# The key-bias term of each query in block B: from a TensorE row product to VectorE sums over row buffers

## The reference

```python
h = film(rmsnorm(x, norm1_w), cond, film1_w, film1_b)
Q = h @ q_w + q_b
K = h @ k_w + k_b
V = h @ v_w + v_b
scores = jnp.einsum('bnd,bmd->bnm', Q, K) * D ** (-0.5)
attn = jax.nn.softmax(scores, axis=-1)
out = jnp.einsum('bnm,bmd->bnd', attn, V)
x = x_in + (out @ proj_w + proj_b)
h = film(rmsnorm(x, norm2_w), cond, film2_w, film2_b)
h = jax.nn.gelu(h @ mlp_w1 + mlp_b1, approximate=False) @ mlp_w2 + mlp_b2
```

## Time and profile before

| | |
|---|---|
| median of 3 runs | 1538.35 us (1538.13 to 1538.81) |
| the profiled execution | 1537.32 us, its span 1535.4 us |
| TensorE busy | 1515.0 us (99%) |
| VectorE, ScalarE, GpSimd busy | 788.4, 592.9, 581.4 us |
| DMA | 117.87 MB, mean 77 GB/s |

### The profile page before, as it was taken

How to read it: one execution, slowest core, us unless ns; L and a number is a source line. 1 busy time by engine, 2 the same in 40 slices (tenths; PEclk the granted TensorE clock), 3 DMA queues, 4 the chain that set the end, 5 groups by cost and what they waited for, 6 DMA issues and landing times.

```text
span 1535.4 us, 24533 instructions
## 1 busy us (share of the span) xinstructions
PE 1515.0 (99%) x8992; PEld 1235.9 (80%) x8992; DVE 788.4 (51%) x1616; ACT 592.9 (39%) x1884; POOL 581.4 (38%) x504
## 2 busy tenths in 40 slices
PE   5999999999999999999999999999999999999999
PEld 4888888888887668888788888888888888888887
DVE  5677777777766675555546342332524233252522
ACT  4656565656554446555554221211212121121210
POOL 5656666676654545443553311021211102121100
PEclk9999999999999999999999999999999999999999
DMA  7122222222126234333343220020201002020100
GB/s 252 63 80 87 80 93 77 96 77 91 58 81 232 71 138 158 97 103 126 122 127 114 69 69 15 1 82 0 75 7 68 14 1 81 0 75 7 55 1 28
DMA packets 60237, 117.87 MB, mean 77 GB/s; under 512 B 6352, under 2 KB 10448, under 8 KB 60144
## 3 DMA queue, kind: packets, MB, share of 16 engines
q1 hardware_dynamic: 60144, 116.65, 22.4%
HBM read 91.33 MB, written 25.30 MB: 76 GB/s over the span
## 4 chain that ended last, share of the span: by engine, by line
PE 97%; POOL 1%; DVE 1%; DMA 1%; SPq 0%; issue 0%
PE bank L587 27%; PE bank L589 27%; PE bank L588 27%; PE bank L666 4%; PE bank L659 2%; PE bank L677 2%; PE bank L963 2%; PE bank L884 1%; PE bank L718 1%; PE bank L709 1%; PE bank L611 1%; PE bank L987 1%; POOL xa L1746 1%; DMA xa<-xt_in 1%; PE bank L906 1%; PE bank L966 0%
## 5 line engine op out<-in xcount | busy, mean ns | idle before, releaser
L1705 DVE CAST g_hi<-gf 128x512 fp32r<-128x512 f32 x128 | 68.7, 537 | 427.1 <-ACT gf L1271 427.1
L1271 ACT ACTIVATE gf<-bank,cols 128x512 f32<-128x512 f32 x128 | 88.3, 690 | 512.6 <-PE bank L589 512.6
L1106 ACT ACTIVATE pa<-bank,neg_max 128x128 f32<-128x128 f32 x512 | 181.7, 408 | 135.5 <-DVE neg_max L1378 135.5
L587 PE MATMUL bank<-w_hi,g_hi 128*128 128x512 f32 x512 | 200.5, 392 | 0.0
L587 PE MATMUL bank<-hb_hi,w_hi 128*128 128x512 f32 x512 | 199.4, 389 | 0.3 <-DVE vb_lo L1294 0.3
L589 PE MATMUL bank<-w_hi,g_lo 128*128 128x512 f32 x512 | 199.4, 389 | 0.0
L588 PE MATMUL bank<-w_lo,g_hi 128*128 128x512 f32 x512 | 199.2, 389 | 0.0
L589 PE MATMUL bank<-hb_hi,w_lo 128*128 128x512 f32 x512 | 199.2, 389 | 0.0
L588 PE MATMUL bank<-hb_lo,w_hi 128*128 128x512 f32 x512 | 199.2, 389 | 0.0
L1781 POOL TENSOR_TENSOR pa<-pa,rec 128x512 f32<-128x512 f32 x128 | 143.2, 1126 | 56.2 <-DVE rec L1401 56.1
L1755 POOL TENSOR_TENSOR xrc<-xrc,b 128x512 f32<-128x512 f32 x32 | 48.7, 1550 | 303.0 <-DMA xrc<-x_dram 302.9
(11 more groups left out here) (201 smaller groups left out, 3132.6 us busy)
## 6 DMA issues: line engine op xcount, KB each, us to landing
rows<-st_dram SPq DMA_DIRECT2D x32, 512.0 KB, 4.3
xb<-x_dram SPq DMA_DIRECT2D x60, 256.0 KB, 2.9
xa<-xt_in SPq DMA_DIRECT2D x32, 256.0 KB, 4.4
xra<-xt_in SPq DMA_DIRECT2D x32, 256.0 KB, 2.7
x_dram<-h SPq DMA_DIRECT2D x32, 256.0 KB, 2.0
xrb<-x_dram SPq DMA_DIRECT2D x32, 256.0 KB, 3.3
stage_w<-w_in SPq DMA_DIRECT2D x16, 512.0 KB, 3.8
x_dram<-xrb SPq DMA_DIRECT2D x32, 256.0 KB, 2.2
```

The lines of the kernel that those rows point to most:

```text
L587: nc.tensor.matmul(dst, w_hi, a_hi, start=start, stop=False)
L1106: last = nc.scalar.activation(pa[:, j, m, :], scores_bank[j][:, m * P:(m + 1) * P], ACT.Exp, bias=neg_max[:, j * C + m:j * C + m + 1], acc ...
L1271: nc.scalar.activation(gf[f % 2][:], bank[f % 2][:], ACT.Gelu, bias=cols[:, B1_COL + f:B1_COL + f + 1])\
L1705: nc.vector.tensor_copy(g_hi[:, r, :], gf[f % 2][:]).then_inc(g_hi_ready, 1)
```

## The change

From group 1 on, `h_u`, the copy to rb and the fifth score product are left out; group 0 keeps them. In their place the key-bias term is summed on VectorE: for sequence t, the row u_t = scale_t * uc (512 numbers) is written to DRAM once (`u_dram`, made in group 0 by four multiplications or sums on VectorE, `u_transpose` on TensorE and a copy on ScalarE), loaded to all partitions by SP into one of four row buffers (`u_row`, 256 KB each), and `query_bias(t)` multiplies it with the normalised input xnb and sums over the row. The shift's part, one constant for a sequence, is in `cst`. `whole_query_bias` adds both before a group's tiles. Behind each reduction one more small instruction adds the term to the bias of the exponential, where it cancels against the maximum. query_bias of tiles 2 and 3 of the next group stands at the end of a group, that of tiles 0 and 1 at m = 2 and 3 of the next h_g. GpSimd's norm_b gets a wait for query_bias of the tile whose xnb it overwrites. The diff, without semaphore names and the raw weights' semaphores:

```diff
@@ -219,6 +219,18 @@
         xrb = run("xrb", [P, GB, D])
         stage_w1_at = run.offset
         stage_w1 = run("stage_w1", [P, 2, C, FF // NG])
+        u_row = run("u_row", [P, GB, D])
+        assert run.offset == stage_w1_at + 16 * kib
+        u_rows = run("u_rows", [NB, D])
+        run = Run(rows_at + 2 * kib)
+        u_tab = run("u_tab", [P, C, NB])
+        u_part = run("u_part", [P, NB, C])
+        u_sum = run("u_sum", [P, 2, NB])
+        cst = run("cst", [P, NB])
+        rq = run("rq", [P, 2, GB])
+        rq_full = run("rq_full", [P, 2, 2, GB])
+        assert run.offset <= rows_at + 4 * kib
+        run = Run(stage_w1_at)
         run.offset = stage_w1_at + 16 * kib
         assert base + run.offset <= 229344
         pb = at("pb", [P, 2, P], F32, tmp_at)
@@ -226,6 +238,7 @@
         ptb_lo = at("ptb_lo", [P, 2, P], F32R, rows_at + kib)
         fv2 = at("fv2", [P, D], F32, vb_at)
         uc_rows = fv1
+        u_junk = at("u_junk", [P, D], BF16, st_at)
         run = Run(R0)
...
@@ -468,6 +483,8 @@
             sp.wait_ge(tp_done, HM * NB)
             load_bx(1, 0)
             load_bx(1, 1)
+            sp.wait_ge(st_rows_made, 3)
+            sp.dma_start(u_dram[:], u_rows[:]).then_inc(st_stored, 16)
             store_x1(NB - 2)
             load_bx(1, 2)
             load_bx(1, 3)
@@ -475,6 +492,7 @@
             for b in range(GB):
                 sp.wait_ge(x1_out[b], 16 * NG)
+            sp.wait_ge(st_stored, 32)
@@ -497,6 +515,12 @@
                 sp.wait_ge(x2_out[b], 16)
                 load_bx(NG, b, x2_dram, b)
+
+            def load_u_row(t):
+
+                wait(sp, rq_made, t - 2 * GB + 1)
+                sp.dma_start(u_row[:, t % GB], u_dram[t:t + 1, :].partition_broadcast(P))\
+                    .then_inc(rows_ld[t % GB // 2], 16)
             def load_w1(i):
@@ -507,6 +531,9 @@
                 ahead = g == NG - 2
                 for b in range(GB - 1):
                     load_bxr(g, b)
+                if not first and not last:
+                    load_u_row(GB * (g + 1) + 2)
+                    load_u_row(GB * (g + 1) + 3)
                 if not first:
                     for b in range(2, GB):
                         if last:
@@ -516,12 +543,18 @@
                     store_x2(g - 1, GB - 1)
                 load_bxr(g, GB - 1)
                 if first:
+                    for b in range(GB):
+                        load_u_row(GB + b)
+                if first:
                     load_w1(0)
                 if last:
                     load_w2(0)
                 else:
                     load_w1(g + 1)
                 store_x2(g, 0)
+                if not last and not ahead:
+                    load_u_row(GB * (g + 2))
+                    load_u_row(GB * (g + 2) + 1)
                 store_x2(g, 1)
                 if not last:
                     for b in range(2):
...
@@ -907,6 +938,14 @@
                                             hb[:, k, :], start=True, stop=True)
                 last.then_inc(br_done, 1)
+            def u_transpose():
+
+                pe.wait_ge(cst_made, 1)
+                for c in range(C):
+                    nc.tensor.transpose(bank[3][0:NB, c * P:(c + 1) * P], u_tab[:, c, :], ident[:])
+                nc.tensor.matmul(bank[2][:, 0:NB], inv_hd[:].broadcast_to([P, P]), u_sum[:, 1, :], start=True,
+                                 stop=True).then_inc(uc_t, 1)
+
             def values_b(g, b):
                 tok = slice(b * P, (b + 1) * P)
@@ -941,7 +980,9 @@
                         transpose_pb(g - 1, GB - 1)
                     if m == 1 and not first:
                         attend_b(g - 1, GB - 1)
-                    if m == 2:
+                    if m == 0 and first:
+                        u_transpose()
+                    if m == 2 and first:
                         h_u(g)
                 if first:
                     pe.wait_ge(wvp_hi_made, C)
@@ -956,15 +997,20 @@
                         pe.wait_ge(bg_free[0], uses_h(g, 2) + 1)
                         pe.wait_ge(bg_free[1], uses_h(g, 3) + 1)
-                        pe.wait_ge(br_copied, g + 1)
+                        if first:
+                            pe.wait_ge(br_copied, 1)
+                            pe.wait_ge(cst_made, 2)
+                            pe.wait_ge(st_rows_made, 3)
+                        pe.wait_ge(hb_copied, g + 1)
                     wait(pe, bexp, t - 1)
                     tok = slice(b * P, (b + 1) * P)
                     for k in range(C):
-                        nc.tensor.matmul(ps_s[b % 2][:, 0:P], tb[:, k, tok], hb[:, k, tok], start=(k == 0),
-                                         stop=False)
-
-                    nc.tensor.matmul(ps_s[b % 2][:, 0:P], rb[:, tok], inv_hd[:].broadcast_to([P, P]), start=False,
-                                     stop=True).then_inc(bs_done, 1)
+                        last = nc.tensor.matmul(ps_s[b % 2][:, 0:P], tb[:, k, tok], hb[:, k, tok], start=(k == 0),
+                                                stop=(k == C - 1 and not first))
+                    if first:
+                        last = nc.tensor.matmul(ps_s[b % 2][:, 0:P], rb[:, tok], inv_hd[:].broadcast_to([P, P]),
+                                                start=False, stop=True)
+                    last.then_inc(bs_done, 1)
                     if b < GB - 1:
                         norm_b(g, b + 1)
                         values_b(g, b + 1)
@@ -1221,11 +1267,12 @@
                 squares_b(g + 1, 0)
                 squares_b(g + 1, 1)
                 if first:
-                    act.wait_ge(uc_made, 1)
+                    act.wait_ge(uc_t, 2)
+                    nc.scalar.activation(u_rows[:], bank[3][0:NB, :], ACT.Identity).then_inc(st_rows_made, 1)
+                    act.wait_ge(br_done, 1)
+                    nc.scalar.activation(rb[:], bank[7][:], ACT.Identity, bias=bqk_sum[:, 1:2]).then_inc(br_copied, 1)
                 else:
                     split_w1(g)
-                act.wait_ge(br_done, g + 1)
-                nc.scalar.activation(rb[:], bank[7][:], ACT.Identity, bias=bqk_sum[:, 1:2]).then_inc(br_copied, 1)
                 squares_b(g + 1, 2)
                 squares_b(g + 1, 3)
                 act.wait_ge(hb_copied, g + 1)
@@ -1572,6 +1619,29 @@
             residual(NB - 1)
+            u0 = uc[:, 0, :]
+            then(nc.vector.tensor_tensor(u_part[:], st_f1[:, :, C:2 * C], u0.unsqueeze(1).broadcast_to([P, NB, C]),
+                                         ALU.mult))
+            then(nc.vector.tensor_reduce(u_sum[:, 0, :], u_part[:], AX.X, ALU.add))
+            then(nc.vector.tensor_scalar(u_sum[:, 1, :], u_sum[:, 0, :], bqk_sum[:, 0:1], None, ALU.add))
+            nc.vector.tensor_tensor(u_tab[:], st_f1[:, :, 0:C].rearrange("p b c -> p c b"),
+                                    u0.unsqueeze(2).broadcast_to([P, C, NB]), ALU.mult).then_inc(cst_made, 1)
+
+            def query_bias(t):
+
+                dve.wait_ge(bxn, t + 1)
+                dve.wait_ge(rows_ld[t % GB // 2], 16 * (NB // 2 + 2 * (t // GB)))
+                wait(dve, rq_made, t - GB)
+                nc.vector.scalar_tensor_tensor(u_junk[:], xnb[:, t % GB], 1.0, u_row[:, t % GB], ALU.mult, ALU.mult,
+                                               accum_out=rq[:, t // GB % 2, t % GB:t % GB + 1]).then_inc(rq_made, 1)
+
+            def whole_query_bias(g):
+
+                dve.wait_ge(rq_made, GB * g)
+                i = g % 2
+                then(nc.vector.tensor_tensor(rq_full[:, i, 0, :], rq[:, i, :], cst[:, GB * g:GB * (g + 1)], ALU.add))
+                then(nc.vector.tensor_scalar(rq_full[:, i, 1, :], rq_full[:, i, 0, :], INV_SQRT_D, None, ALU.mult))
+
             def end_a(m):
                 if m == 0 or m == 2:
@@ -1627,6 +1697,11 @@
                         residual_b(g - 1, GB - 1)
                     if first:
                         end_a(m)
+                    if first and m == 0:
+                        dve.wait_ge(uc_t, 2)
+                        nc.vector.tensor_scalar(cst[:], bank[2][:, 0:NB], float(HD), None, ALU.mult).then_inc(cst_made, 1)
+                    if not first and not last and m >= 2:
+                        query_bias(GB * (g + 1) + m - 2)
                     if m < 2:
                         mean_square(g + 1, m, bssq, bxn, bvar)
                     if m == 1 and not first:
@@ -1634,14 +1709,21 @@
                 mean_square(g + 1, 2, bssq, bxn, bvar)
                 mean_square(g + 1, 3, bssq, bxn, bvar)
                 low_v(g, 0)
+                if not first:
+                    whole_query_bias(g)
                 for b in range(GB):
                     t = GB * g + b
                     dve.wait_ge(bs_done, t + 1)
                     nc.vector.tensor_reduce(neg_max[:, 2 * (b % 2):2 * (b % 2) + 1], ps_s[b % 2][:, 0:P], AX.X, ALU.max, negate=True)\
                         .then_inc(braw, 1)
```

(26 more changed lines are left out.)

4 lines of the change are left out of this document (2 added, 2 removed).

## The result

| | before | after |
|---|---|---|
| median | 1538.50 us (5 runs, 1538.13 to 1538.81) | 1545.19 us (5 runs, 1544.45 to 1546.51) |
| ratio | | 1.0048, 95% interval 1.0036 to 1.0059 |
| the profiled execution, its span | 1537.32, 1535.4 us | 1545.19, 1543.3 us |
| TensorE, VectorE busy | 1515.0, 788.4 us | 1507.1, 819.6 us |
| DMA | 117.87 MB | 125.27 MB |

The change costs 6.7 us. The time is inside the range (1530 to 1547.5); the forecast was +1.7, within what a measurement can tell, and the change came out slower.

What follows compares the result with a forecast made beforehand. TensorE was taken to bound the kernel, with loops of other engines 0.4 us a group behind. +3.0 (group 0 into 1), five periods of 32.5 against 32.55, -0.7 and -0.3 gave +1.7: 1540.0 us, range 1530 to 1547.5.

Steps and rivals of the forecast that it cites:

- within, 0.42: Outcome class: total time within some 0.2% (3.1 us) of the kernel before, so not told from no change; chance 0.42.
- loop B: Block B, GpSimd's rstd, xnb and add_bias holding up hb_lo of tile 1: 30.5 us a group, 32.5 with the change.
- loop A: Block B, exponentials, xb load, squares, next_h, reduction and back: 30.7 us a group, 31.8 with the small instructions.
- The bound moves off TensorE: Block B: TensorE's gain is lost to the loops, period 32.55 to 32.5 us, TensorE idle some 2; chance 0.35.
- 0.37 and 1.45: Idle us in loop A: 0.37 before vb_hi, waiting for TensorE; 1.45 over the usual 4.61 between exponentials 0 and 1.
- (a): Groups 1 to 7, one more small VectorE instruction between each reduction and exponential: 0.18 us each.
- (b): whole_query_bias, two small VectorE instructions before a group's first reduction: 0.36 us.
- Last group and end: Group 7 has no query_bias or row load: period into it 31.8 us, -0.7; the end behind it -0.3.
- TensorE remains the bound: Rival: the exponentials can be ahead by more than found, so block B keeps TensorE's gain: -11.8, 1526.5 us; chance 0.10.
- Half lost: Rival: row loads cost xb nothing or hb_lo gets in between add_bias; loop A decides at 31.8: 1536.5 us; chance 0.25.
- Half rate: Rival: query_bias's STT with accumulator takes 1.4 us and decides at a group's tail: 1547.7 us; chance 0.15.
- Row loads and GpSimd's port: Rival: xnb of tile 1 stretched 0.5 us, loads at upper bound; period 33.1 to 33.3, 1543 to 1544 us; chance 0.15.

Runs made afterwards that it cites:

- e11: Changed kernel without repeated row loads, memsets for the sums, no small instructions; the work of group 0 stays: 1529.16 us, -9.5 against before.
- e8: Changed kernel with small instructions kept, row buffers loaded in group 0 only and memsets for the sums: 1539.53 us, +2.1 against before.
- e3: Changed kernel with each query_bias sum replaced by a memset of its result; row loads and small instructions stay: 1543.93 us, +6.5 against before.
- e2: Changed kernel with row buffers loaded in group 0 only and used in all groups; sums and small instructions stay: 1540.50 us, +2.0 against before.
- e7: Changed kernel with its row loads, but memsets for the sums and no extra small instructions: 1533.32 us, -4.1 against before.
- e9: Changed kernel with the row product h_u computed again in every group, its result unused: 1546.85 us, +8.2 against before.
- e6: Kernel before without row product, its copy and fifth score product in all eight groups, nothing in their place: 1528.55 us, -8.9 against before.
- e1: Kernel before without row product and fifth score product from group 1 on, nothing in their place: 1528.58 us, -9.9 against before.
- e4: Changed kernel without whole_query_bias and with one scaling behind each reduction; row loads and sums stay: 1535.74 us, -2.8 against before.
- e12: Kernel before, products out in all groups, 1/sqrt(D) folded into the copy to tb, the scaling behind each reduction gone: 1525.85 us, -12.2 against before.
- e10: Changed kernel with the first of the two small instructions behind each reduction done twice: 1554.94 us, +16.3 against before.

## Why the prediction was right or wrong

The number fell into a range of 17.5 us, which took in three of the five rivals and nearly all of a fourth; that it fell inside says little. The forecast itself was 5 us too fast, and its most likely class (within, 0.42) did not come. The prediction's sum, sorted by the change's parts, against the pairs of kernels that differ by one part alone:

| part | predicted | measured |
|---|---|---|
| products out, with the work in group 0 | six periods at 30.7, -11.1; end -0.8; u_transpose +0.7: -11.2 | -9.5 (e11) |
| small instructions | 1.08 in six periods, 0.1 and 0.5 at the ends: +7.1 | +9.5, +10.6, +11.6 |
| row loads | loop B 0.7 over loop A, five periods: +3.5 | +4.4 (e8, e3), +4.7 (e2, after), +5.4 (e11, e7) |
| sums | group 0 into 1: +2.2 | -0.1, +0.2, +1.3 |
| sum | +1.6 | +6.7 |

- **The bound moves off TensorE**: right, and the main reason why the change doesn't gain. TensorE's idle 1.2 us ahead of h_g and up to 2.2 ahead of `transpose_pb` weren't there before, vb_hi(0) has no wait left, and 8.3 us of TensorE put back cost 1.5 (e9). I had placed the idle ahead of `transpose_pb` and `attend_b` only; in six groups it also stands ahead of h_g(0), for hb_hi and hb_lo of tile 3, which I hadn't followed.
- **Loop A's length without additions**: 30.7 was too short. It came from taking all idle time out of one group's loop (0.37 and 1.45). The kernels without additions show 30.7 to 31.4 in all groups but one each, mean 31.2 to 31.4 (e6, e1, e11). Over six periods 0.5 to 0.7 too little is 3 to 4 us; of the whole term 1.7 is missing. Part of it is that the 1.45 was not idle time to take out whole: in e1 hb_lo of tile 1 began 3.01 behind that of tile 0 (group 3) instead of 3.82, but still took 1.02 to 1.32 us beside add_bias in five of the six groups, and exponential 0 to 1 took 5.02 in the mean and not 4.61.
- **Small instructions**: the term of the sum that was mis-sized most, by 2.4 to 4.5 us. (a) took 0.25, not 0.18: the scaling now has two operands from SBUF and takes 0.21 instead of 0.15, and 0.16 and the gaps come on top. (b) took 0.39 in four of the seven groups and 0.77 to 0.89 in the three where one of its two instructions lay beside GpSimd. That makes 1.39 a group instead of 1.08; on the 31.0 of most groups of e1 it gives 32.4, and e8 shows 32.4. The rest is what they meet when they come later: in group 4 of after, L1642 took 0.65 and L1726 0.56 beside GpSimd (below).
- **Row loads**: they were sized nearly right in sum and put in the wrong loop. The forecast had them delay GpSimd's row and so hb_lo of tile 1 (loop B). But hb_lo of tile 1 took 0.69 to 0.98 in groups 1 to 7 of after, not the 1.34 of the earlier trace rows (0.85 in the group shown), and exponential 0 to 1 fell from 6.06 to 5.02. Loop B let go; the loads are felt in loop A, where squares of tiles 2 and 3 come late. Group 4 shows it most; SP's queue, ScalarE, and VectorE and GpSimd behind them:

```profile
704.05 3.33 SPq L480 DMA_DIRECT2D xb<-x_dram  x2
...
710.18 0.63 ACT L1174 ACTIVATE junk<-xb 128x512 bf16<-128x512 f32 x1 [6.57 <-issue]
...
714.18 0.65 DVE L1642 TENSOR_TENSOR rq_full<-rq,cst 128x4 f32<-128x4 f32 x1
714.76 0.58 POOL L1857 TENSOR_TENSOR rstd<-ve,neg_half 128x1 f32<-128x1 f32 x1
...
715.64 0.56 DVE L1726 TENSOR_TENSOR neg_max<-neg_max,rq_full 128x1 f32<-128x1 f32 x1
```

  Squares of tile 2 were 6.1 us behind their load there, GpSimd's rstd and xnb came as late and lay beside VectorE's small instructions; the period was 34.10.
- **Sums**: 0.83 each was right (665.49 to 666.31, 0.82), and in a steady group they cost next to nothing, as said. Group 0 into 1 was forecast at 2.2 for them; the traces show 2.2 (36.20 - 34.02, after and e3) and 2.6 (e4 and e7) where rows are loaded, and 0.3 (e2 and e8) where not. The medians have only -0.1 to 1.3. How the two go together is open: each trace is one execution, and the executions of e3 alone spread over 4.2 us.
- **The four first row loads: nothing**: borne out (e11, which has them, is 0.4 us over e1, which hasn't). But the next pair, rows 8 and 9, was in no step of the sum. Group 0 into 1 is 1.05 and 1.07 longer with the loads (e3 over e8, e7 over e11). Row 9 takes the buffer of row 5, so its load waits on SP for query_bias(5), and ends up right in front of xb. After, SP's queue, ScalarE and TensorE, 590 to 604 us:

```profile
593.18 4.04 SPq L522 DMA_DIRECT2D u_row<-u_dram  x2
...
598.38 0.95 SPq L480 DMA_DIRECT2D xb<-x_dram  x2
...
603.17 0.63 ACT L1174 ACTIVATE junk<-xb 128x512 bf16<-128x512 f32 x1 [2.65 <-issue]
...
595.77 0.48 PE L620 MATMUL bank<-hb_hi,g_hi_b 128*128 128x512 f32 x1 [0.93 <-ACT hb_hi L1235]
602.45 0.50 PE L620 MATMUL bank<-vb_hi,ptb_hi 128*128 128x512 f32 x1 [0.84 <-DVE ptb_lo L1341]
```

  Squares of tile 0 came 4.8 us behind the issue of xb instead of 2.8. The change adds a wait on SP here, in front of xb, and the prediction named neither it nor what is queued behind it.
- **Last group and end**: forecast -0.7 and -0.3; period 32.43 into group 7, -0.1 against 32.56 but +0.5 against before's own 31.92, and -0.95 at the end. TensorE waits 1.76 there where the earlier trace rows has 0.32.
- **Rivals.** TensorE remains the bound (1526.5): no. Half lost (1536.5): no; loop A alone, without loads, is 32.7 to 32.8 and not 31.8 (e2, e8). Half rate (1547.7): near in time and false in its cause, since a sum takes 0.83. Row loads and GpSimd's port (1543 to 1544, period 33.1 to 33.3): nearest in cause, and the mean period is 33.07; it lacked the group 0 transition and the dearer small instructions.

## What to carry to other kernels

An engine that is busy for 99% of its time can be 1.3 us of 32.6 away from not being the bound: before its work is moved, take it out alone, without any substitute, since that run (here -9.9 of 14.8 us) is the ceiling of every change that only puts other work in its place. An instruction of 0.15 to 0.2 us on the serial stretch between reduction and exponential cost more here than a sum of 0.83 us that stands in a gap; count what is moved by the place and not by the duration. A term that cancels in the softmax is best not computed (e6, -8.9 us). A scale folded into a copy that is made anyway shortened each tile's stretch by 0.19 us (e12), though the periods did not follow.

## What was unexpected of the hardware

- A SCALAR_TENSOR_TENSOR with accumulator over two fp32 tiles in SBUF, 128x512, with bf16 output, took 683 ns in the median and its read-out 81 ns more. Section 7 of the Trainium skill's page Vector Engine (DVE) Microarchitecture Reference, by which it would run at half throughput, isn't borne out here: the measurement decides.
- The port shared with GpSimd holds up small VectorE instructions as much as large ones: 128x1 additions of 0.16 us took 0.56 and 1.25, a 128x4 one 0.65 instead of 0.15, and a 128x512 sum 1.77 instead of 0.68, each beside GpSimd. The 128x1 addition of e10 and the 128x512 sum each lost 1.09, so the loss doesn't shrink with the size. The scaling with one number from each of two tiles (L1725) never lost any: 213 to 216 ns in all 28. The Trainium skill's SBUF — State Buffer, in its section on the two separate sides, has it that a VectorE instruction with two SBUF inputs waits while GpSimd holds the port they share. The trace agrees for the additions and the sum. But a 128x4 scaling with one tile in (L1643) once took 0.55 instead of 0.17 as well, 0.18 us behind the start of GpSimd's xnb; two inputs can't be its reason. And that section has the port held for GpSimd's whole instruction: beside add_bias (1.26 us) that was so, but beside xnb (1.57 us) the small ones were through 0.7 us behind its start.
- In nearly every kernel one of the six later periods is 0.6 to 2.5 us longer than its neighbours (before 33.20 into group 6; e1 32.50, e8 34.62, e2 34.54 into group 5); in before and e8 the first xb load of that group lands 4.2 to 4.6 us behind its issue instead of 2.8. No run here says what delays it.
